# Causal attention rounds on GpSimd: the order of the feed-forward's square and gate, a mask, and the last step of the operand split

## The chip, the cores and the metric

The kernel runs on one core of a Trainium2 chip. The metric is the device time of one execution in microseconds (us), the median of several runs. The engines are TensorE (PE; PEld is its weight load), VectorE (DVE), ScalarE (ACT), GpSimd (POOL) and SyncE (SP), which here only issues transfers.

## The reference

An encoder-like block on x of 16 sequences, 256 tokens and 128 channels:

```python
x = x + 0.5 * L0_ffn(layernorm(x))      # r = sigmoid(xr @ W_r'), k = relu(xk @ W_k')**2, out = r * (k @ W_v')
x = x + L0_attn(layernorm(x))           # causal attention, 16 heads of 8 channels, softmax with clip and epsilons
x = x + 0.5 * L0_ffn(layernorm(x))
x = x + 0.5 * L1_ffn(layernorm(x))      # 8 experts, top 2
x = x + L1_attn(layernorm(x))           # 3 steps of a refined attention
x = x + 0.5 * L1_ffn(layernorm(x))
```

In L0_ffn, xr and xk are mixtures of each token with the one before it: x_prev + mu * (x - x_prev). Only the first three lines bear on the change: they are worked out together, sequence by sequence.

## The kernel before, in words

The first three lines of the block run as 16 **causal rounds**, one for each sequence n, with eight steps each, one for each pair of heads (`causal_round` in the program of every engine, called by `causal_steps`: rounds 0, 1 and 12 to 15 written out, 2 to 11 as a hardware loop of two rounds). Round n holds the attention of sequence n, the second feed-forward of sequence n - 2, the first feed-forward of sequence n + 3, and the preparation of operands of sequences n + 1 and n + 2. Each engine runs its own list strictly in order; what ties the lists together are semaphores. So the order in which the Python function of an engine calls its helpers is the order of its queue, and that order is written out by hand.

For one pair of heads TensorE computes the scores twice: `row_scores` (L1736, mask product L1747 and score products L1752) into ps_q, from which VectorE takes row maxima (`row_maxima`, L2622), and `causal_scores` (L1757) into ps_k, which ScalarE exponentiates (`causal_exps`, L1290). GpSimd then sets what lies above the diagonal to zero (`causal_keep`, L935, an affine select at L940). Behind every second pair TensorE multiplies with the values (`causal_values`, L1768, products L1778 and L1781), once the masks of its two pairs are done.

**The feed-forward** of one sequence passes through all engines. VectorE normalises (`ln_apply`, L2576), TensorE transposes (`tokens_t`, L1682), ScalarE copies to y_t, GpSimd takes the difference of neighbouring tokens (`mix_step`, L875), VectorE makes the two mixtures (`mix_inputs`, L2592 and L2593), TensorE multiplies (`ffn_hidden`, L1696 and L1698), ScalarE writes kr, the relu of k (L1192), and the logarithm for the sigmoid's denominator (L1194 to L1199). GpSimd squares kr (`mix_square`, L879, waits for kr) and adds the two parts of the logarithm (`mix_gate`, L884, waits for the Ln of L1199). TensorE multiplies the square with W_v (`ffn_out`, L1704, waits for the square), ScalarE's last exponential (L1203) waits for the gate, VectorE forms the product (`mix_gated`, L2599), GpSimd adds it to x (`mix_add`, L889). A flag `first` stands for the first feed-forward (rounds 0 to 12), `second` for the second (rounds 2 to 15).

**The operand split.** Queries and keys of the next sequence are needed as three bf16 parts. ScalarE rounds qk32 to part 0, GpSimd does the rest: `causal_parts` (rest = qk32 - part 0, L916; part 1 = rest rounded, L920) and `causal_last_parts` (part 2 = rest - part 1, L924). The last one raises `parts_ready`, for which SP waits in `causal_operands`: SP then issues one transfer of the query parts to DRAM (scr_q, L707), three of the key parts (scr_x, L710), and behind waits for those, six back into q_st (`query_halves`, L597) and two into k_st (`key_halves`, L605). TensorE's `row_scores` for pair 0 of round n + 1 waits for all eight of these (`fast_operands_in`). ScalarE's next write into parts, late in the round, waits for the outward transfers. Splits take place in rounds 1 to 14 (`parts_next`).

On VectorE the list around the change is: maxima of the fourth pair, `causal_normalise` (L2662 to L2668, ends with o_tok, which TensorE transposes behind the values of the second group), maxima of the fifth pair, `mix_inputs` of the second feed-forward (waits for GpSimd's step L875), `mix_gated` of the first (waits for TensorE's and ScalarE's results), `middle_normed` (y of sequence n + 2, L2576), maxima of the sixth pair. TensorE's transposes of that y are L1682 into ps_m.

Of the kernel before, what the change touches and what calls it, by code (L numbers as in the profile page):

```python
# [73 lines left out]
def macaron_kernel(nc, a, out):  # L74
    ctx = ExitStack()
    with ctx:
# [39 lines left out]
        def sem(name):  # L116
            if name not in made:
                made[name] = ctx.enter_context(nc.semaphore(name))
            return made[name]
# [271 lines left out]
        def within(n, low, high):  # L391

            return not isinstance(n, int) or low <= n <= high
# [13 lines left out]
        def mix1(f):  # L407
            return place(mix_order, 1, f, (2, -5))

        def mix2(b):  # L410
            return place(mix_order, 2, b, (2, 6))

        def norm1(f):
            return place(norm_order, 1, f, (3, -6))
# [4 lines left out]
        def norm3(b):  # L419
            return place(norm_order, 3, b, (3, 10))  # L420
# [393 lines left out]
        def _(pool):  # L814
# [53 lines left out]
            def hold():  # L868

                pool.sem_inc(sem("held"), 1)  # L870


            def mix_step(i, l):
                pool.wait_ge(sem("T_ytc"), l + 1)
                pool.tensor_tensor(dy[:, :], y_t[:, 1:T + 1], y_t[:, 0:T], ALU.subtract).then_inc(sem("F_dy"), 1)  # L875

            def mix_square(i):
                pool.wait_ge(sem("F_kr"), i + 1)
                pool.tensor_tensor(ka[:, :], kr[:, :], kr[:, :], ALU.mult).then_inc(sem("F_ka"), 1)  # L879

            def mix_gate(i):

                pool.wait_ge(sem("F_ln"), i * 3 + 3)
                pool.tensor_tensor(er[:, :], er[:, :], rec[:, :], ALU.add).then_inc(sem("F_sum"), 1)  # L884

            def mix_add(i, b):
                pool.wait_ge(sem("F_gated"), i + 1)
                hold()
                pool.tensor_tensor(x[:, b, :], x[:, b, :], gated[:, :], ALU.add).then_inc(sem("F_x"), 1)  # L889
# [23 lines left out]
            def causal_parts(f):  # L913

                pool.wait_ge(sem("part_hi"), f + 1)
                pool.tensor_tensor(rest[:, :, :], qk32[:, :, :], parts[:, :, 0, :], ALU.subtract)\  # L916
                    .then_inc(sem("part_rest"), 1)
                pool.wait_ge(sem("part_rest"), f + 1)
                hold()
                pool.tensor_copy(parts[:, :, 1, :], rest[:, :, :]).then_inc(sem("part_mid"), 1)  # L920

            def causal_last_parts(f):
                pool.wait_ge(sem("part_mid"), f + 1)
                pool.tensor_tensor(parts[:, :, 2, :], rest[:, :, :], parts[:, :, 1, :], ALU.subtract)\  # L924
                    .then_inc(sem("parts_ready"), 1)

            def causal_values(n, p):
                if not isinstance(n, int) or n >= 2:
                    pool.wait_ge(sem("fast_values"), (n - 1) * NGV + 2)
                pool.wait_ge(sem("G_vc"), n + 1 + 1)  # L930
                hold()
                pool.tensor_copy(v_heads(p)[:, :, :, 0:HD], v_tok[:, :, :, :].rearrange("p t (a s) d -> p (t a) s d", s=2))\
                    .then_inc(sem("fast_v"), 1)

            def causal_keep(n, hp):  # L935
                g, j = hp * 2 // HG, hp * 2 % HG
                pool.wait_ge(sem("fast_exp"), n * HP + hp + 1 + 2)
                hold()
                e = e_buf[g % 2][:, j:j + 2, 0:2 * P].rearrange("p u (c q) -> p u c q", c=2)
                pool.affine_select(out=e, in_=e, compare_op=ALU.is_ge, fill=0.0, base=0,  # L940
                                   pattern=[[0, 2], [0, 2], [1, P]], channel_multiplier=-1)\
                    .then_inc(sem("causal_kept"), 1)

            def causal_round(n, p, half):
                first, second, after = within(n, 0, B - 4), within(n, 2, B), within(n, 0, B - 2)
                parts_next = within(n, 1, B - 2)
                causal_keep(n, 0)
                if first:
                    mix_step(mix1(n + 3), norm1(n + 3))
                causal_keep(n, 1)  # L950
                if parts_next:
                    causal_parts(n + 1)
                causal_keep(n, 2)
                if parts_next:
                    causal_last_parts(n + 1)
                if first:
                    mix_square(mix1(n + 3))
                    mix_gate(mix1(n + 3))
                causal_keep(n, 3)
                if second:  # L960
                    mix_step(mix2(n - 2), norm3(n - 2))
                causal_keep(n, 4)
                if first:
                    mix_add(mix1(n + 3), n + 3)
                causal_keep(n, 5)
                if second:
                    mix_square(mix2(n - 2))
                    mix_gate(mix2(n - 2))
                causal_keep(n, 6)
                if after:  # L970
                    causal_values(n + 1, 1 - p)
                causal_keep(n, 7)
                if second:
                    mix_add(mix2(n - 2), n - 2)
# [19 lines left out]
            causal_parts(1)  # L994
            causal_last_parts(1)
            causal_steps(pool, causal_round)
            ffn(mix2(B - 2), norm3(B - 2), B - 2)
            ffn(mix2(B - 1), norm3(B - 1), B - 1)
# [2702 lines left out]
```

## Time and profile before

| | us |
|---|---|
| median of 3 runs | 1375.23 |
| lowest, highest | 1371.81, 1378.19 |
| the profiled execution | 1369.53 |
| its span, first to last instruction | 1367.8 |
| busy: PE, DVE, ACT, POOL | 1217.5, 920.0, 842.2, 533.9 |
| granted TensorE clock, mean share of full | 0.966 |

The busy times are sums over the whole span. The kernel has stages with different limits, so they say little about one stage; for that the waits and the timelines of a stretch are read. A timeline row has the start in us from the span's start, the duration, the engine, the line and the operation; in brackets stands how long the engine had been idle, and what released it. Neighbouring durations can overlap by some hundredths.

### The profile page before, as it was taken

Reading aid. Unit: us, or ns where it says so; the run is one execution under the profiler, and the core shown is the slowest. Engines: PE = TensorE matmul, PEld = TensorE weight load, DVE = VectorE, ACT = ScalarE, POOL = GpSimd, SP = SyncE. Lnnn points to the kernel's source line nnn. Section 1 sums busy time; section 2 is a strip of 40 time slices with the busy share of each in tenths; the row PEclk is TensorE's granted clock in tenths of the full one; section 3 lists DMA queues with packets and bytes.
Section 4 is the critical chain, followed back from the end, with each engine's and each line's share of the span. In section 5 each row is a group of like instructions: output and inputs, shape, how many; then the busy total and the mean of one; then the engine's idle time right before and its main releaser. Section 6 shows DMA issues by size and latency. Waiting matters only on the chain. (4 is left out here: it accounts for less than half of the span.)

```text
span 1367.8 us, 36731 instructions
## 1 busy us (share of the span) xinstructions
PE 1217.5 (89%) x12275; PEld 781.6 (57%) x12275; DVE 920.0 (67%) x2874; ACT 842.2 (62%) x1549; POOL 533.9 (39%) x817
## 2 busy tenths in 40 slices
PE   4689899898759999999889988999899997999998
PEld 3456566566537777777544433444344443767876
DVE  3578888887746874677677745666766665677444
ACT  3467777776433344443677877899787885333543
POOL 6366766766430040401344433344333331032344
PEclk9799999999959999999999999999999999999999
DMA  6323323324204022111545544445434441001332
GB/s 162 93 66 93 97 58 104 92 64 106 53 7 139 3 76 84 55 32 52 142 120 155 151 126 113 144 137 141 126 111 126 122 119 39 1 28 41 102 115 85
DMA packets 113582, 125.77 MB, mean 92 GB/s; under 512 B 14988, under 2 KB 90020, under 8 KB 113450
## 3 DMA queue, kind: packets, MB, share of 16 engines
q1 hardware_dynamic: 110378, 117.82, 30.6%
q0 software_dynamic: 3072, 6.30, 1.5%
q8 instruction: 69, 1.13, 0.3%
q14 instruction: 63, 0.52, 0.1%
HBM read 79.89 MB, written 44.05 MB: 91 GB/s over the span
## 5 line engine op out<-in xcount | busy, mean ns | idle before, releaser
L1469 ACT ACTIVATE e_buf<-ps_q 128x1024 f32<-128x1024 f32 x192 | 196.9, 1026 | 58.0 <-PE ps_q L2194 57.7
L2207 PE MATMUL ps_o<-e_buf,v_st 128*32 128x256 f32 x3072 | 210.7, 393 | 5.1 <-POOL v_st L1081 4.2
L1469 ACT ACTIVATE e_buf<-ps_k 128x1024 f32<-128x1024 f32 x192 | 197.0, 1026 | 7.5 <-PE ps_k L2194 7.4
L2054 PEld LDWEIGHTS ps_o<-w,e_buf 128*128 128x128 f32 x1280 | 152.2, 193 | 13.1 <-issue 12.0
L2054 PE MATMUL ps_o<-w,e_buf 128*128 128x128 f32 x1280 | 158.4, 277 | 0.0
L2622 DVE TENSOR_REDUCE mx<-ps_q 128x10 f32<-128x640 f32 x128 | 104.9, 820 | 45.0 <-PE ps_q L1752 44.1
L1290 ACT ACTIVATE e_buf<-ps_k 128x768 f32<-128x768 f32 x128 | 103.0, 805 | 46.2 <-PE ps_k L1764 45.3
L2207 PEld LDWEIGHTS ps_o<-e_buf,v_st 128*32 128x32 f32 x3072 | 81.5, 110 | 76.6 <-issue 40.3
L940 POOL TENSOR_SCALAR_AFFINE_SELECT e_buf<-e_buf 128x512 f32<-128x512 f32 x128 | 85.6, 669 | 89.8 <-ACT e_buf L1290 86.9
L1385 ACT ACTIVATE e_buf<-ps_q,b_t 128x512 f32<-128x512 f32 x80 | 54.6, 685 | 90.5 <-PE ps_q L2046 86.7
L1385 ACT ACTIVATE e_buf<-ps_k,b_t 128x512 f32<-128x512 f32 x80 | 54.0, 685 | 71.0 <-PE ps_k L2046 67.6
L2194 PE MATMUL ps_q<-q_st,k_st 64*128 64x256 bf16 x768 | 76.6, 278 | 19.9 <-DMA q_st<-scr_q 15.8
L2194 PE MATMUL ps_k<-q_st,k_st 64*128 64x256 bf16 x768 | 75.4, 275 | 5.4 <-ACT e_buf L1469 3.1
L1039 POOL DMA_INDIRECT slots_in<-heads_out,vp_all x40 | 39.7, 991 | 101.0 <-DVEq L3526 89.6
L2194 PEld LDWEIGHTS ps_q<-q_st,k_st 64*128 64x128 bf16 x768 | 22.3, 94 | 99.2 <-ACT e_buf L1469 62.6
L1088 POOL TENSOR_TENSOR rest<-qk,parts 128x256 f32<-128x256 f32 x48 | 32.6, 680 | 112.9 <-DVE parts L3141 112.9
L2046 PE MATMUL ps_q<-mix,w 128*128 128x512 f32 x144 | 70.1, 610 | 2.4 <-issue 2.4
L1747 PE MATMUL ps_q<-mask_d,ident_b 64*64 64x128 bf16 x512 | 57.6, 232 | 13.6 <-DVE mx L2622 8.4
L2046 PE MATMUL ps_k<-mix,w 128*128 128x512 f32 x144 | 68.0, 594 | 0.0
L3125 DVE COPY y_t<-ps_m 128x256 f32<-128x256 f32 x48 | 20.3, 423 | 70.0 <-PE ps_m L1682 69.7
L2898 DVE SCALAR_TENSOR_TENSOR e_buf<-ps_o,lexp,e_buf 128x128 f32<-128x128 f32 x160 | 44.8, 342 | 33.0 <-PE ps_o L2054 30.2
L1752 PE MATMUL ps_q<-k_st,q_st 64*64 64x256 bf16 (+3 forms) x1024 | 67.0, 235 | 0.0
(392 smaller groups left out, 2746.5 us busy)
## 6 DMA issues: line engine op xcount, KB each, us to landing
k_st<-scr_x SPq DMA_DIRECT2D x128, 256.0 KB
q_st<-scr_q SPq DMA_DIRECT2D x256, 96.0 KB
scr_q<-parts SPq DMA_DIRECT2D x64, 192.0 KB, 2.0
scr_x<-parts SPq DMA_DIRECT2D x48, 192.0 KB, 2.0
q_st<-scr_q SPq DMA_DIRECT2D x128, 64.0 KB
slots_in<-heads_out SPq DMA_DIRECT2D x3, 1536.0 KB
slots_out<-heads_out SPq DMA_DIRECT2D x18, 256.0 KB
heads_out<-slots_in SPq DMA_DIRECT2D x15, 256.0 KB
```

What stands on the lines that cost most here:

```text
L940: pool.affine_select(out=e, in_=e, compare_op=ALU.is_ge, fill=0.0, base=0, pattern=[[0, 2], [0, 2], [1, P]], channel_multiplier=-1)\
L1290: act.activation(e_buf[g % 2][:, hp * 2 % HG:hp * 2 % HG + 2, 0:3 * P], ps_k[:, :, 0:3 * P], ACT.Exp, bias=SHIFT).then_inc(sem("fast_exp"), 1)
L1385: act.activation(h_sb[e % 2][:, f, :], bank, ACT.Relu, bias=b1_t[:, j:j + 1])\
L1469: act.activation(e_buf[g % 2][:, hp * 2 % HG:hp * 2 % HG + 2, :], (ps_q, ps_k)[hp % 2][:, :, :], ACT.Exp).then_inc(sem("fast_exp"), 1)
L1747: mm(o[at, own[0]:own[1] + 1:own[1] - own[0], :], ident_b[at, at], mask_d[at, :, :], start=True, stop=False, tile_position=(u * RH, u * RH ...
L1752: last = mm(ps_q[at, bank, seg * RH:(seg + j + 1) * RH], q[at, hp, j * RH:(j + 1) * RH], k[at, hp, 0:(j + 1) * RH], start=False, stop=True ...
L2046: mm(bank, w1[:, e, f * P:(f + 1) * P], mixed(m, u)[:, :], start=True, stop=True)\
L2054: last = mm(ps_o[:, e % 2, t * P:(t + 1) * P], h_sb[e % 2][:, f, t * P:(t + 1) * P], w2[:, e * NF + f, :], start=f == 0, stop=f == NF - 1)
L2194: last = mm(bank[:, u, t * T:(t + 1) * T], k_st[p][at, h, t * P:(t + 1) * P], q_st[p][at, h, :], start=True, stop=True, tile_position=(64 ...
L2207: last = mm(ps_o[at:at + VW, p, low:low + T], v_st[p][:, kt, h, :], e_buf[g % 2][:, j, kt * T:(kt + 1) * T], start=g == 0 and kt == 0, sto ...
L2622: red(mx[:, hp, :, :], ps_q[:, :, 0:SEGS * RH].rearrange("p b (s k) -> p b s k", k=RH), AX.X, ALU.max)\
L2898: last = stt(acc[u][:, t, :], ps_o[:, e % 2, t * P:(t + 1) * P], gate[u][:, t, e:e + 1], acc[u][:, t, :], ALU.mult, ALU.add)
```

## The change

In the rounds with a split (1 to 14) GpSimd's list between the third and the fourth pair's mask, and behind the latter, is put in another order. Before: mask 3, last part, square, gate, mask 4, step. After: mask 3, square, gate, mask 4, last part, step. No instruction is added, removed or altered, and no other engine's program changes. In rounds 13 and 14, which have no first feed-forward, mask 4 now stands ahead of the last part; in rounds 0 and 15, which have no split, nothing moves.

```diff
--- before.py
+++ after.py
@@ -951,12 +951,12 @@
                 if parts_next:
                     causal_parts(n + 1)
                 causal_keep(n, 2)
-                if parts_next:
-                    causal_last_parts(n + 1)
                 if first:
                     mix_square(mix1(n + 3))
                     mix_gate(mix1(n + 3))
                 causal_keep(n, 3)
+                if parts_next:
+                    causal_last_parts(n + 1)
                 if second:
                     mix_step(mix2(n - 2), norm3(n - 2))
                 causal_keep(n, 4)
```

## Rows read from the trace of the kernel before

**Rows 1.** Waits, 60 to 320 us: engine, line, releaser; us in total, times, longest.

```profile
PE ps_m L1704 <- POOL mix L879: 16.6, 12, 1.6
...
PEld ps_m L1682 <- DVE y L2576: 4.5, 18, 0.3
```

**Rows 2.** GpSimd's timeline in round 7: start, duration, line, operation [idle before, releaser].

```profile
202.72 0.68 POOL L940 TENSOR_SCALAR_AFFINE_SELECT e_buf<-e_buf 128x512 f32<-128x512 f32 x1
203.37 1.15 POOL L924 TENSOR_TENSOR parts<-rest,parts 128x512 bf16<-128x512 f32 x1
204.48 0.85 POOL L879 TENSOR_TENSOR mix<-mix 128x256 f32<-128x256 f32 x1
205.29 0.90 POOL L884 TENSOR_TENSOR mix<-mix 128x256 f32<-128x256 f32 x1
206.15 0.82 POOL L940 TENSOR_SCALAR_AFFINE_SELECT e_buf<-e_buf 128x512 f32<-128x512 f32 x1
206.94 0.60 POOL L875 TENSOR_TENSOR mix<-y_t 128x256 f32<-128x256 f32 x1
207.98 0.64 POOL L940 TENSOR_SCALAR_AFFINE_SELECT e_buf<-e_buf 128x512 f32<-128x512 f32 x1 [0.43 <-ACT e_buf L1290]
...
211.61 0.61 POOL L879 TENSOR_TENSOR mix<-mix 128x256 f32<-128x256 f32 x1 [0.70 <-ACT mix L1192]
213.06 0.73 POOL L884 TENSOR_TENSOR mix<-mix 128x256 f32<-128x256 f32 x1 [0.83 <-ACT mix L1199]
```

**Rows 3.** TensorE's timeline in round 7, and where rounds 8, 11 and 14 start.

```profile
205.47 0.71 PE L1704 MATMUL ps_m<-w_t,mix 128*128 128x128 f32 x4 [1.36 <-POOL mix L879]
...
207.03 0.64 PE L1781 MATMUL ps_o<-e_buf,v_st 128*32 128x256 f32 x8
...
209.79 0.44 PE L1682 MATMUL ps_m<-ident,y 128*128 128x128 f32 x2
...
216.65 0.24 PE L1747 MATMUL ps_q<-mask_d,ident_b 64*64 64x128 bf16 x2
...
278.67 0.24 PE L1747 MATMUL ps_q<-mask_d,ident_b 64*64 64x128 bf16 x2
...
339.22 0.24 PE L1747 MATMUL ps_q<-mask_d,ident_b 64*64 64x128 bf16 x2
```

**Rows 4.** VectorE's timeline in round 7.

```profile
204.45 0.41 DVE L2662 TENSOR_TENSOR corr<-s_du,vs 128x256 f32<-128x256 f32 x1
...
205.65 0.83 DVE L2668 TENSOR_TENSOR o_tok<-corr,s_rec 128x256 f32<-128x256 f32 x1
206.84 0.82 DVE L2622 TENSOR_REDUCE mx<-ps_q 128x10 f32<-128x640 f32 x1 [0.36 <-PE ps_q L1752]
207.58 0.48 DVE L2592 SCALAR_TENSOR_TENSOR mix<-mix,cols,y_t 128x256 f32<-128x256 f32 x1
...
209.15 0.59 DVE L2576 TENSOR_SCALAR y<-x,mv,rstd 128x128 f32 x2
```

**Rows 5.** ScalarE's timeline in round 7: Ln of the gate, exponential of pair four.

```profile
203.62 0.42 ACT L1199 ACTIVATE mix<-mix 128x256 f32<-128x256 f32 x1
203.94 0.79 ACT L1290 ACTIVATE e_buf<-ps_k 128x768 f32<-128x768 f32 x1
```

**Rows 6.** VectorE's timeline behind the last round: L2668 with GpSimd idle.

```profile
388.80 0.42 DVE L2668 TENSOR_TENSOR o_tok<-corr,s_rec 128x256 f32<-128x256 f32 x1
```

**Rows 7.** Stretches of 0.25 us: busy by engine, PEclk, share of DMA engines, GB/s.

```profile
213.25:213.50 0.25, 0.25 (x6) 0.16 (x8) 0.14 (x2) 0.25 (x1) 0.25 (x1) 1.00 0.03 0
276.00:276.25 0.25, 0.25 (x12) 0.12 (x6) 0.00 (x0) 0.24 (x1) 0.25 (x1) 1.00 0.01 0
338.00:338.25 0.25, 0.25 (x5) 0.25 (x4) 0.24 (x1) 0.25 (x1) 0.00 (x0) 1.00 0.08 33
726.25:726.50 0.25, 0.25 (x12) 0.09 (x4) 0.24 (x1) 0.25 (x1) 0.08 (x2) 1.00 0.02 0
```

**Rows 8.** TensorE's timeline in the later attention stage: a start behind transfers.

```profile
727.48 0.40 PE L2194 MATMUL ps_q<-q_st,k_st 64*128 64x256 bf16 x4 [0.66 <-DMA q_st<-scr_q]
```

## The prediction

> **What bounds the kernel now.** The change touches only the causal rounds, 16 of some 20.7 us each in a span of 1367.8 us, so I read that stretch alone. First the waits there: between 60 and 320 us TensorE stands idle 16.6 us in 12 pieces until GpSimd's square (L879) is done, and right behind it stands a second, much smaller wait, 4.5 us in 18 pieces, for VectorE's normed rows y [rows 1]. The first is the wait that the edit aims at; the second tells how near the next limit is. Then the engines one by one through one round of the loop (n = 7; round 8 starts at 216.65 and round 11 at 278.67, so 20.67 us each [rows 3]; pairs are counted from one, the third mask is `causal_keep(n, 2)`). GpSimd works without a gap from the third mask at 202.72 to the second step at 207.54: mask, last part, square, gate, mask, step [rows 2]. TensorE waits 1.36 us for the square, starts the value product at 205.47, the values of group two at 207.03, is at the transposes of y at 209.79, and from there on it is busy without a recorded wait to the next round's first scores at 216.65 [rows 3]. VectorE normalises until 206.48, reduces the scores at 206.84, starts mix_inputs at 207.58, which is 0.04 us after GpSimd's step ended, and has y ready at 209.74, 0.05 us before TensorE uses it [rows 2 to 4]. So what sets the second half of the round is a chain: GpSimd's unbroken row up to the step, mix_inputs, mix_gated, y, transposes. TensorE's wait for the square lies beside this chain, and ends in it.
>
> **The square and the gate, moved ahead.** The work on GpSimd is the same six instructions. The square can start at 203.37 instead of 204.48. Alone it takes 0.61 us, beside VectorE's work 0.85 [rows 2]; here it falls beside a reduction, where the last part took no longer either, so I take 0.61: end 203.98, and TensorE starts about 204.15, 1.3 us sooner. The gate needs ScalarE's Ln, which ends at 204.04 [rows 5]; other engines start 0.04 to 0.14 behind an end that they wait for (step to mix_inputs, square to product [rows 2 to 4]), so 204.12: GpSimd's row gets a new gap of 0.14. Gate 0.73 (at 213.06) to 0.90, I take 0.73, as it starts before VectorE's product at 204.45: end 204.85. The mask of pair four needs the exponential that ends at 204.73 [rows 5], so no wait; 0.64 (as the third's 0.68) to 0.82, I take 0.82: end 205.65.
>
> **The last part, moved behind the mask.** It starts at 205.6 and takes 1.15 to 1.35 (the other two-input operations got 0.17 to 0.24 longer beside VectorE), I take 1.26: end 206.86 instead of 204.52, **2.34 us later**. With everything short it is 0.61 + 0.14 + 0.73 + 0.64 = 2.1 later, with everything long 0.85 + 0.14 + 0.90 + 0.82 + 0.2 = 2.9. The step of the second feed-forward comes next: 0.60 to 0.78, end 207.5 to 207.65 against 207.54.
>
> **VectorE beside it.** Its product L2668 takes 0.42 alone [rows 6] and 0.83 when GpSimd is at work beside it [rows 4]; 205.65 plus 0.41 is 206.06, close to where the gate ends, so I read it as waiting for GpSimd's running instruction. In the new order that instruction is the long last part: L2668 would end near 207.1 instead of 206.48, the reduction near 207.9 instead of 207.66, and mix_inputs would start 0.1 to 0.25 late. Against that, the fifth mask, which starts at 207.98 today [rows 2] because its exponential is late, could run right behind the step: then it lies beside less of mix_inputs, which is 1.6 us from its start to y's [rows 4], and that takes back some tenths. I set this at 0 to 0.1 a round, between ends of -0.3 (no overlap anywhere) and +0.3. **So y does not come sooner**, and TensorE's 1.3 us turns into waits for the reduction (208.0) and for y (209.8). Expected gain of the moved square: nothing in rounds 2 to 12; in round 1, which has no second step, up to 1 us, if the next operands are there.
>
> **The transfers behind the last part.** This is the term that I think decides. parts_ready starts SP's twelve transfers: one to scr_q, three to scr_x, six back to q_st, two to k_st. TensorE's first scores of the next round wait for the last eight. No row shows the end of that wait, since it was never the last. I bound it: in round 7 the engines stop moving data at 213.3 [rows 7], 8.8 us behind the last part. How much later the wait is free shows in a later stage, where the same six and two transfers are the last thing awaited: data stops near 726.3, and TensorE starts at 727.48 [rows 7, 8], 1.15 us on. So the operands were usable at about 214.45 and used at 216.65: 2.2 us to spare, against a shift of 2.34. In round 10 data stops near 276.05 (usable 277.2) and the scores start at 278.67: 1.45 to spare [rows 3, 7]. The rest of the rounds lie between, most near the first. Lateness is then 0.15 to 0.9 a round, I take 0.3 on the mean of rounds 1 to 12; it is not won back, as the whole loop hangs on that start: 12 x 0.3 = 3.6 us. Round 1's possible gain is lost to the same wait. In rounds 13 and 14 there is no square; only the mask goes ahead, and the last part comes 0.8 to 1.0 later. Round 13 has nothing to spare: data stops near 338.2, usable 339.35, scores at 339.22 [rows 3, 7]; it pays 0.8. Round 14 is as the first, with room. ScalarE's next write to parts waits for the outward transfers alone, and comes only behind the seventh pair (GpSimd's gate at 213.06 lies ahead of it [rows 2]); at 2.3 us later they are still in by then, so I put it at nothing. If that cover went, the split of the round after next would start late, with most of a round to spare.
>
> The Trainium skill (DMA: Bandwidth & Descriptors, "Anatomy of one DMA", which is on GpSimd's path) puts the fixed part of a transfer at some 2.0 us and says that most of it is the write receipt. By that figure the operands would be usable at 215.3 and round 7 late by 1.0 us, as an estimate 12 us in all, which is the lower half of rival (a) below; the rows show 1.15 for the same transfers, and the sum goes by them.
>
> **Sum.** Square and gate 0; y chain 0.05 x 11 = 0.5; operands 3.6 + 0.8 = 4.4; round 1 another -0.6 before its operands bind. That is +4.3 us on the profiled execution's 1369.5 us, which lies 5.7 below the median of the runs; carried to the median, 1375.2 + 4.3 = **1379.5 us**. A measurement of this kernel can tell about 0.5% (6.9 us) from no change.
>
> **Rivals.**
> (a) *Operands truly late, slower.* The place is the first scores of each round. If the last part shifts by 2.9 (all of GpSimd's work beside VectorE's) against 2.2 to spare, or by 2.34 with the spare time of all rounds nearer to round 10's 1.45, each of 13 rounds pays 0.6 to 0.9 us, and up to 1.4 with both: +8 to +15, 1383 to 1390 us. It decides from a mean lateness of 0.53 us a round. For it: spare and shift are within 0.2 of each other, so every error on that side counts in full; against it: the row at 727.48. Chance 0.28.
> (b) *Nothing binds.* Shift 2.1, spare 2.2: operands just in time, y as before, +0 to -3 us: 1372 to 1377. Chance 0.24.
> (c) *The wait was the bound, faster.* If TensorE's 1.3 us passes through to y, 12 x 1.3 = 15.6 less: 1360 us. For it speaks only the size of the wait; against it the 0.04 us between step and mix_inputs and the 0.05 between y and the transposes. It needs the operands in time too. Chance 0.07, partial gains of over 0.5% included.
> My forecast (y chain unchanged, operands late by a little) has 0.41, with a range of its own of 1377 to 1383.
>
> **How the numbers follow.** Faster by over 0.5% is (c), 0.07. Slower by over 0.5% is (a), 0.28. The rest, 0.65, is within. The range runs from (b)'s lower part, with a margin for the 3 us by which single runs differ, to the middle of (a): 1370 to 1388.
>
> **What would show it.** Right: TensorE's wait for L879 gone or under 0.3 us; a wait of about 1 us before the transposes of y instead; mix_inputs still starting within 0.2 us behind L875; the last part ending 2.1 to 2.9 later in the round; a new wait "DMA q_st or k_st" before the first L1747 of most rounds, 0.1 to 0.9 us each; a period of 20.7 to 21.2. Wrong: a period under 20.4 (then y was not the limit), or no wait for operands at all with the last part 2.3 later (then the spare time was misread).

## The result, and the profile after

The median went from 1372.49 us (13 runs, 1366.87 to 1378.19) to 1381.40 us (13 runs, 1371.22 to 1388.51): ratio 1.0066, 95% interval 1.0043 to 1.0090, so 9 us slower, between 6 and 12. The profiled execution took 1376.49 us (span 1374.8) against 1369.53 (span 1367.8); both lie below the medians, the one after by 4.9. The forecast was 1379.5, in a range of 1370 to 1388. The three runs whose median of 1375.23 stands ahead of the prediction are among the 13. Here and below, "ratio" is the ratio on record with its 95% interval; it can differ by up to a quarter of a per cent from the quotient of two medians.

First the waits of the kernel after, 60 to 325 us (engine, line, releaser; us in total, times, longest). They answer to [rows 1].

```profile
PEld ps_q L1747 <- issue: 27.5, 75, 2.2
...
PE ps_m L1682 <- DVE o_tok L2668: 8.6, 12, 0.7
...
PE ps_q L1747 <- DMA k_st<-scr_x: 5.4, 8, 2.0
...
PE ps_m L1682 <- DVE y L2576: 3.7, 12, 0.8
...
PEld ps_m L1704 <- POOL mix L879: 0.7, 2, 0.5
...
PE ps_m L1704 <- POOL mix L879: 0.3, 1, 0.3
```

TensorE's 16.6 us for the square are down to 0.3 in one piece (1.0 with the weight loads), most of it in the stretch up to 100 us. In their place stand 8.6 us for o_tok and 3.7 for y, in every round, and a wait that the kernel before did not have: 5.4 us in 8 pieces until k_st has landed. The weight load ahead of the same line grew with it ("issue", longest 0.5 before and 2.2 now).

GpSimd's timeline in round 7 of the kernel after, which answers to [rows 2]. The round starts at 199.49; it started at 196.00 before, so 3.49 is taken off for a comparison.

```profile
206.75 0.61 POOL L879 TENSOR_TENSOR mix<-mix 128x256 f32<-128x256 f32 x1
207.37 0.73 POOL L884 TENSOR_TENSOR mix<-mix 128x256 f32<-128x256 f32 x1
208.16 0.71 POOL L940 TENSOR_SCALAR_AFFINE_SELECT e_buf<-e_buf 128x512 f32<-128x512 f32 x1
208.84 1.32 POOL L924 TENSOR_TENSOR parts<-rest,parts 128x512 bf16<-128x512 f32 x1
210.13 0.79 POOL L875 TENSOR_TENSOR mix<-y_t 128x256 f32<-128x256 f32 x1
210.87 0.63 POOL L940 TENSOR_SCALAR_AFFINE_SELECT e_buf<-e_buf 128x512 f32<-128x512 f32 x1
```

VectorE's and TensorE's timelines of the same round, answering to [rows 4] and [rows 3].

```profile
209.18 1.26 DVE L2668 TENSOR_TENSOR o_tok<-corr,s_rec 128x256 f32<-128x256 f32 x1
210.37 0.81 DVE L2622 TENSOR_REDUCE mx<-ps_q 128x10 f32<-128x640 f32 x1
211.10 0.68 DVE L2592 SCALAR_TENSOR_TENSOR mix<-mix,cols,y_t 128x256 f32<-128x256 f32 x1
...
212.44 0.59 DVE L2576 TENSOR_SCALAR y<-x,mv,rstd 128x128 f32 x2
```

```profile
207.49 0.71 PE L1704 MATMUL ps_m<-w_t,mix 128*128 128x128 f32 x4
...
210.50 0.44 PE L1682 MATMUL ps_m<-ident,o_tok 128*128 128x128 f32 x2 [0.72 <-DVE o_tok L2668]
211.33 0.24 PE L1747 MATMUL ps_q<-mask_d,ident_b 64*64 64x128 bf16 x2 [0.39 <-DVE mx L2622]
...
213.08 0.44 PE L1682 MATMUL ps_m<-ident,y 128*128 128x128 f32 x2 [0.26 <-DVE y L2576]
...
220.25 0.24 PE L1747 MATMUL ps_q<-mask_d,ident_b 64*64 64x128 bf16 x2 [0.24 <-DMA k_st<-scr_x]
```

From the round's own start, before and after:

| | before | after |
|---|---|---|
| square (L879) ends | 9.33 | 7.87 |
| last part (L924) ends | 8.52 | 10.67 |
| step (L875) ends | 11.54 | 11.43 |
| o_tok (L2668) ends | 10.48 | 10.95 |
| mix_inputs (L2592) starts | 11.58 | 11.61 |
| y (L2576) ends | 13.74 | 13.54 |
| next round starts | 20.65 | 20.76 |

The square comes 1.46 us sooner, and y comes 0.2 sooner: the gain stops between the two. The last part comes 2.15 later, and the next round now waits for the operands. In the records of the transfers one can read when the last of the eight that TensorE waits for has landed. Before, that was 1.78, 2.98, 1.96, 2.36, 2.29, 1.97, 2.38, 2.52, 2.33, 1.61, 2.16, 2.78, 0.39 and 2.84 us ahead of the next round's first matmul, for rounds 1 to 14. After, it is 0.14 to 0.25 in all of these rounds but 6 (1.62) and 14 (2.96): the operands have become what starts the round, and TensorE starts 0.14 to 0.25 us behind their landing.

Next rounds 1 to 3, 6 and 7 of the kernel after as stretches (length; busy PE, PEld, DVE, ACT, POOL; PEclk, share of the DMA engines, GB/s), then 13 and 14.

```profile
71.53:92.69 21.16, 17.03 (x243) 11.22 (x243) 16.52 (x45) 13.58 (x31) 11.45 (x16) 1.00 0.31 86
92.69:114.35 21.66, 18.72 (x254) 12.72 (x255) 17.68 (x48) 15.04 (x37) 14.25 (x20) 1.00 0.30 84
114.35:136.01 21.66, 18.73 (x254) 12.73 (x255) 17.62 (x49) 15.05 (x37) 14.22 (x20) 1.00 0.33 84
...
177.50:199.49 21.99, 20.21 (x255) 13.69 (x255) 17.77 (x48) 14.90 (x37) 14.41 (x21) 0.92 0.28 80
199.49:220.25 20.76, 18.73 (x256) 12.73 (x256) 17.44 (x51) 15.23 (x38) 14.24 (x21) 1.00 0.30 85
...
324.04:343.04 19.00, 16.48 (x244) 11.29 (x244) 14.63 (x41) 12.51 (x28) 11.39 (x17) 1.00 0.34 95
343.04:365.38 22.34, 19.12 (x237) 12.40 (x236) 16.20 (x47) 10.68 (x24) 10.60 (x16) 0.77 0.30 81
```

And of the kernel before, rounds 1 to 3, 13 and 14.

```profile
71.60:91.75 20.15, 18.20 (x243) 11.69 (x242) 15.37 (x44) 12.79 (x28) 11.56 (x16) 0.92 0.33 90
91.75:113.36 21.61, 19.82 (x256) 13.34 (x255) 16.81 (x49) 15.16 (x37) 13.09 (x19) 0.92 0.30 84
113.36:134.00 20.64, 18.71 (x255) 12.69 (x254) 17.76 (x50) 15.23 (x37) 14.36 (x21) 1.00 0.32 88
...
320.58:339.22 18.64, 16.56 (x244) 11.30 (x244) 14.27 (x41) 12.50 (x28) 11.35 (x17) 1.00 0.39 97
339.22:359.99 20.77, 17.07 (x237) 11.48 (x237) 15.49 (x47) 10.69 (x24) 10.63 (x16) 0.92 0.34 87
```

A common round is hardly longer (rounds 7 to 11: 20.71 on the mean against 20.66), but rounds 1 to 3 together are 64.48 against 62.40, and of the three of after, all at full clock, two are almost a whole microsecond over the common round. Stretches at half clock (1.2 GHz; PEclk 0.92 is one of 3.4 us in a round) fall in rounds 1, 2 and 14 before, in 6 and 14 after; a round with one is 1.0 to 1.3 us longer. Round 15 starts at 365.38 against 359.99: 5.4 of the span's 7.0 us arise in the causal rounds. Rounds 6 and 14, the two of after in which the operands were not late, give 2.9 of these 5.4: both have half clock, round 14 for 10.2 us where it had 3.4 before. So this one profile does not by itself show that late operands cost the time; the experiments do. Of the other 1.6 us, 0.9 arise in round 15, which has a stretch at half clock of 6.8 us where the kernel before has one of 3.4 (both have a longer one at its end); the rest lies in later stages, which the change does not touch.

### The profile page after: what moved, and what is told of

Same layout as the page of the kernel before. It is cut to its first block and busy times, and to the rows that moved or that the text cites. A ratio compares the mean times of both kernels' runs of the same rounds, so it can differ in the third digit from the quotient of the medians.

```text
span 1374.8 us, 36731 instructions
## 1 busy us (share of the span) xinstructions
PE 1219.7 (89%) x12275; PEld 783.1 (57%) x12275; DVE 923.1 (67%) x2874; ACT 840.1 (61%) x1549; POOL 532.4 (39%) x817
## 3 DMA queue, kind: packets, MB, share of 16 engines
q8 instruction: 70, 1.15, 0.4%
## 5 line engine op out<-in xcount | busy, mean ns | idle before, releaser
L2194 PE MATMUL ps_q<-q_st,k_st 64*128 64x256 bf16 x768 | 76.7, 278 | 21.4 <-DMA q_st<-scr_q 17.4
L1747 PE MATMUL ps_q<-mask_d,ident_b 64*64 64x128 bf16 x512 | 57.9, 232 | 22.4 <-DVE mx L2622 11.7
L3125 DVE COPY y_t<-ps_m 128x256 f32<-128x256 f32 x48 | 20.4, 424 | 71.4 <-PE ps_m L1682 71.0
```

Of the source, the lines that this page charges most:

```text
L1747: mm(o[at, own[0]:own[1] + 1:own[1] - own[0], :], ident_b[at, at], mask_d[at, :, :], start=True, stop=False, tile_position=(u * RH, u * RH ...
L2194: last = mm(bank[:, u, t * T:(t + 1) * T], k_st[p][at, h, t * P:(t + 1) * P], q_st[p][at, h, :], start=True, stop=True, tile_position=(64 ...
```

## The experiments

The theory going in: late operands. The loss is the operand transfers, which start 2.15 us later, and the square's wait was worth nothing, because GpSimd's list up to the step, mix_inputs and y bound the round. The rivals: a stretched product (the loss is VectorE's L2668, 0.83 before and 1.26 us after, and what follows it), and an eaten gain (the square's gain is real, and the transfers take it back and more). A third rival, that the changed order brings more stretches at half clock, has no run of its own; the clock records speak to it in part, as said below. e1 to e4 ran on one chip with the kernel before at 1370.26 us. e6 to e13 ran on another, on which the later stages take longer (in e12 round 15 starts at 359.82, and the span is 1442.3), with the kernel before at 1447.16 (e6 to e9) and 1441.83 (e10 to e13); each ratio is to the kernel before on its own chip.

### e1_square_first: the square sooner, the last part nearly where it was

```diff
                 causal_keep(n, 2)
+                if first:
+                    mix_square(mix1(n + 3))
                 if parts_next:
                     causal_last_parts(n + 1)
                 if first:
-                    mix_square(mix1(n + 3))
                     mix_gate(mix1(n + 3))
```

> Edit: before's order, with the square alone moved ahead of the last part (mask 3, square, last part, gate, mask 4, step). Theory 'operands late' (T): TensorE's wait for the square falls from 16.6 us to under 5, the last part ends only 0.6 to 0.85 us later and the spare time before each round's first scores (1.5 us or more in rounds 1 to 12, round 13 unchanged) still covers it; the step L875 ends when it did, so y and the round stay: period 20.6 to 20.7, ratio to before 0.998 to 1.002. Rival 'the wait was the bound': 1.1 us a round less, ratio 0.990 or lower.

Measured: 1370.97 us, ratio 1.0007 (0.9988 to 1.0026). Its round 7 starts at 194.54. GpSimd's timeline:

```profile
201.91 0.61 POOL L879 TENSOR_TENSOR mix<-mix 128x256 f32<-128x256 f32 x1
202.48 1.15 POOL L924 TENSOR_TENSOR parts<-rest,parts 128x512 bf16<-128x512 f32 x1
203.59 0.91 POOL L884 TENSOR_TENSOR mix<-mix 128x256 f32<-128x256 f32 x1
```

VectorE's:

```profile
202.99 0.93 DVE L2663 TENSOR_TENSOR corr<-s_du,vs 128x256 f32<-128x256 f32 x1
...
204.81 0.74 DVE L2669 TENSOR_TENSOR o_tok<-corr,s_rec 128x256 f32<-128x256 f32 x1
205.47 0.81 DVE L2623 TENSOR_REDUCE mx<-ps_q 128x10 f32<-128x640 f32 x1
```

and TensorE's:

```profile
202.66 0.71 PE L1705 MATMUL ps_m<-w_t,mix 128*128 128x128 f32 x4
...
205.33 0.64 PE L1782 MATMUL ps_o<-e_buf,v_st 128*32 128x256 f32 x8 [1.19 <-POOL e_buf L940]
...
208.42 0.44 PE L1683 MATMUL ps_m<-ident,y 128*128 128x128 f32 x2 [0.44 <-DVE y L2577]
```

The value product starts 8.12 us into the round instead of 9.47, with no wait, and the transposes of y start at 13.88, where they were at 13.79. TensorE waits for the fourth mask instead (1.19 us; it had no recorded wait there), and then for y (0.44). The round is 20.74. VectorE shows why y does not come sooner. Before, it stood idle for 0.36 us ahead of its reduction for the fifth pair (the fifth reduction from here on), until TensorE's scores came [rows 4]. Here the scores are early, but the first product of `causal_normalise` runs under the last part and takes 0.93 us instead of 0.41, the products end 0.53 later in the round, and the reduction follows them with no idle time. So the square's 1.35 us are gained on TensorE and lost again before y. Late operands are not in play from round 2 on (they land 1.2 to 1.9 us ahead of the next start in rounds 2 to 11); only the start of round 2 waits for them. So there is no gain in the loop that the transfers could have eaten.

### e2_transfers_late: the order before, and SP also waits for the fourth mask

```diff
             def causal_operands(f, p, half):
                 sp.wait_ge(sem("parts_ready"), f + 1)
+                if not isinstance(f, int) or f >= 2:
+                    sp.wait_ge(sem("causal_kept"), (f - 1) * HP + 4)
```

> Edit: before's order on GpSimd, but SyncE's wait for parts_ready is joined by a wait for the round's fourth mask (2.45 us behind the last part's end), so that only the operand transfers start later, by about what the change makes them later. T: the loss of the change appears with nothing else altered, +4 to +10 us, ratio 1.003 to 1.008, waits 'DMA' before the first L1747 of most rounds. Rival 'VectorE beside the last part' (L2668 stretched to 1.26 us, o_tok and the reduction late): nothing of it is in this kernel, ratio 1.000 within 0.1%.

Measured: 1376.32 us, ratio 1.0055 (1.0035 to 1.0075). Its waits, 60 to 325 us:

```profile
PE ps_m L1706 <- POOL mix L881: 17.0, 12, 1.6
...
PE ps_q L1749 <- DMA k_st<-scr_x: 5.3, 9, 1.5
```

All compute instructions stand in the order of the kernel before (the square's wait is back, 17.0), and yet the same wait for k_st appears, 5.3 against the change's 5.4, and the same loss. The operands land 20.3 to 21.3 us into a round, the changed kernel's 20.4 to 21.4. With VectorE undisturbed this is the late start of the transfers alone; the stretched product isn't needed for the loss.

### e3_before_mask: the last part behind the gate, but ahead of the fourth mask

```diff
                 causal_keep(n, 2)
-                if parts_next:
-                    causal_last_parts(n + 1)
                 if first:
                     mix_square(mix1(n + 3))
                     mix_gate(mix1(n + 3))
+                if parts_next:
+                    causal_last_parts(n + 1)
                 causal_keep(n, 3)
```

> Edit: square and gate moved ahead as in the change, but the last part left in front of the fourth mask (mask 3, square, gate, last part, mask 4, step). The last part ends about 1.5 us later than before. T: the spare time of 1.5 to 2.8 us covers it in nearly all rounds, so ratio 0.999 to 1.002, with landings just in time in rounds 1 and 10. Rival 'VectorE beside the last part': L2668 still meets a longer GpSimd instruction, and half of the loss stays, ratio 1.003.

Measured: 1372.64 us, ratio 1.0030 (1.0012 to 1.0049), more than was expected. The last part ends 10.13 into the round, 1.6 later than before. In the profiled execution the operands of rounds 2 to 11 still land 0.4 to 0.9 us ahead of the next start, one round of the stretch waits for k_st (1.3 us, ahead of round 2), and the period is 20.68. So this profile does not show the loss that the median shows. With so little to spare, a landing that is late by a few tenths counts, and landings vary by more than that (9.65 to 10.55 behind the last part in one execution of the kernel before). That other executions have such landings is argued, not shown, and other executions may as well differ in their stretches at half clock.

### e4_fewer: the change, with four query transfers back instead of six

```diff
+            def query_fewer(p, landed):
+                for u in range(2):
+                    sp.dma_start(q_st[p][64 * u:64 * u + 48, 0:HP, :].rearrange("r h t -> r (h t)"),
+                                 bass.AP(scr_q.tensor, p * 3 * PLANE + u * HP * T, [[0, 2], [H * T, 24], [1, HP * T]]))\
+                        .then_inc(landed, 16)
...
-                query_halves(p, sem(f"fast_operands_in_{p}"))
+                query_fewer(p, sem(f"fast_operands_in_{p}"))
```

> Edit: the changed kernel, but the six transfers back into q_st are four in the causal rounds (the first two copies of the parts in one transfer), the same bytes. SyncE issues two fewer at 0.39 us each. T: operands land 0.4 to 0.8 us sooner and most of the loss goes: ratio to before 1.000 to 1.003, against the change's 1.0066. Rival 'VectorE beside the last part': the loss stays, 1.006. Rival 'bytes, not issues, set the chain': landings unmoved and the loss stays too; the two are told apart by when the data stops.

Measured: 1490.52 us, ratio 1.0875 (1.0842 to 1.0909): a miss by a wide margin. TensorE waits 52.8 us for k_st:

```profile
PE ps_q L1757 <- DMA k_st<-scr_x: 52.8, 8, 7.8
```

The transfers between 200 and 218 us, as tenths of the 16 engines in 40 slices of 0.45 us, and what they moved:

```profile
DMA  0499995017123099988401111111111110000000
GB/s 0 127 311 325 339 337 163 0 18 164 46 100 109 36 264 273 191 164 200 109 27 46 55 55 55 55 55 55 46 55 46 55 36 18 0 0 0 0 0 0
```

Behind the burst runs a tail of some 12 slices at a tenth of the engines and 55 GB/s, which is 5.4 us. A tenth is about 2 of 16, and the new transfers have a source whose outermost dimension is 2. The Trainium skill (DMA: Bandwidth & Descriptors, "Why a DMA increments its semaphore by 16 and not by 1") says that such a transfer uses the largest number of engines, up to 16, that divides the outermost dimension of both sides: here 2. The trace agrees with its 0.1. Joining transfers this way makes them narrow.

### e6_keys_early: the change, with two of three outward key transfers sent behind part 1

```diff
+                sp.wait_ge(sem("part_mid"), f + 1)
+                hold()
+                key_part(0)
+                key_part(1)
                 sp.wait_ge(sem("parts_ready"), f + 1)
...
-                for j, n in enumerate(PARTS):
-                    sp.dma_start(scr_x[f].rearrange("(i c t) -> c i t", c=C, t=T)[:, 3 * j:3 * j + n, :],
-                                 parts[:, 1, j, :].unsqueeze(1).broadcast_to([P, n, T])).then_inc(sem("k_parts_out"), 16)
+                key_part(2)
```

> Edit: the changed kernel, but SyncE issues the first two of the three outward key transfers as soon as their parts are there (behind L920, a wait for part_mid), and only scr_q and the third behind the last part. Same transfers, same bytes. T: two issues of 0.53 us leave the chain behind the last part, so operands land 0.8 to 1.1 us sooner (9.8 becomes about 8.8 us behind the last part), the spare time turns from 0 to about 1 us in the loop, and the loss of the change goes: ratio to before 0.999 to 1.002, no wait 'DMA' before L1747 but in single rounds. Rival 'the loss sits on GpSimd and VectorE': ratio stays 1.005 to 1.007.

Measured: 1452.67 us, ratio 1.0033 (1.0018 to 1.0048), where the change itself gives 1.0065 on the same chip (e11). GpSimd's list is the changed one, so VectorE is disturbed as there; only transfers moved. The operands land 9.1 to 9.8 us behind the last part instead of 9.7 to 10.8, and the wait for k_st falls from 8 pieces to one:

```profile
PE ps_q L1752 <- DMA k_st<-scr_x: 1.6, 1, 1.6
```

By the two ratios half of the loss is back, though their intervals overlap. The gain of 0.5 us a round in the landing was half of what I had expected, and so was the effect (0.999 to 1.002). What remains is not explained by this profile: round 15 starts at 363.92, 4.1 us later than in e12, and rounds 12 to 14, whose operands land 1.8 to 3.0 us ahead, are longer than e12's by 5.2 us together, with 13.7 us at half clock against 3.4.

### e7_keys_first, e8_step_first, e9_old_order

e7 is e6 with the two transfers into k_st issued ahead of the six into q_st:

```diff
-                sp.wait_ge(sem("parts_out"), f * 16 + 32)
-                hold()
-                query_halves(p, sem(f"fast_operands_in_{p}"))
                 sp.wait_ge(sem("k_parts_out"), f * 48 + 96)
                 hold()
                 key_halves(p, f, sem(f"fast_operands_in_{p}"))
+                sp.wait_ge(sem("parts_out"), f * 16 + 32)
+                hold()
+                query_halves(p, sem(f"fast_operands_in_{p}"))
```

> Edit: as e6_keys_early, and the two large transfers into k_st are issued ahead of the six into q_st. T: the data of the large two then moves under the issues of the six; landings 7 to 8 us behind the last part, 2 us or more to spare, ratio 0.998 to 1.001; no further gain over e6 but in rounds whose landing varied. If the period of the loop stays at 20.66 with 2 us to spare, the limit is the chain of GpSimd's step, mix_inputs and y.

Measured: 1457.27 us, ratio 1.0074 (1.0047 to 1.0102), a miss: the operands land 10.0 to 11.2 behind the last part, later than in e6. TensorE's wait is now for q_st:

```profile
PE ps_q L1752 <- DMA q_st<-scr_q: 10.5, 10, 3.0
```

The group that is issued last is the one that TensorE waits for. In this order the queries stand behind SP's wait for the last outward key transfer, which is a likely cause, not a tested one; the first inward issue comes 2.6 us behind the last part in round 7 against 2.2 in e6, which is less than half of the delay.

e8 puts the step ahead of the last part in e7 (mask 3, square, gate, mask 4, step, last part), to test whether the step is what y waits for:

```diff
                 causal_keep(n, 3)
-                if parts_next:
-                    causal_last_parts(n + 1)
                 if second:
                     mix_step(mix2(n - 2), norm3(n - 2))
+                if parts_next:
+                    causal_last_parts(n + 1)
```

> Edit: as e7_keys_first, and on GpSimd the step of the second feed-forward stands ahead of the last part (mask 3, square, gate, mask 4, step, last part). Theory 'y chain' (the round's second limit is GpSimd's step -> mix_inputs -> y): the step ends about 1.3 us sooner, mix_inputs starts behind the reduction, y comes 0.3 to 0.5 us sooner, period 20.2 to 20.4, ratio 0.995 to 0.998. Rival: period unchanged at 20.66, ratio 1.000.

Measured: 1471.24 us, ratio 1.0175 (1.0143 to 1.0208), a miss. The step ends 1.3 us sooner in a round of the loop, mix_inputs starts 0.5 sooner and y ends 0.2 sooner than in the changed kernel. So it is VectorE's own list that mix_inputs follows: in every version read (before, after, e1, e8) it starts some 0.08 us ahead of the recorded end of the fifth reduction. In the kernel before, the step ended within 0.12 us of that, so its rows could not tell the two apart. The last part ends 0.75 us later still (11.42 in a round) and the wait for operands nearly doubles against e7:

```profile
PE ps_q L1752 <- DMA q_st<-scr_q: 19.5, 11, 2.5
```

This is the late operands again, at a greater shift. VectorE's timeline of e8 in round 8, which starts at 227.55, shows what mix_inputs then follows:

```profile
237.88 0.81 DVE L2627 TENSOR_REDUCE mx<-ps_q 128x10 f32<-128x640 f32 x1
238.61 0.64 DVE L2597 SCALAR_TENSOR_TENSOR mix<-mix,cols,y_t 128x256 f32<-128x256 f32 x1
239.17 0.85 DVE L2598 SCALAR_TENSOR_TENSOR mix<-mix,cols,y_t 128x256 f32<-128x256 f32 x1
```

The reduction ends at 238.69 and mix_inputs runs right behind it; its second half now takes 0.85, as it lies under the fifth mask (238.92 to 239.74), where it took 0.47 in e1.

e9 is the order of before with e7's transfers.

> Edit: before's order on GpSimd with the transfers of e7_keys_first. T: operands 4 to 5 us to spare, which nobody needs: ratio 0.998 to 1.001, the only round that can gain is 13 (0.25 to spare before). A gain of over 0.3% would mean that landings cost before's kernel something in most runs that its one profile does not show.

Measured: 1449.19 us, ratio 1.0008 (0.9990 to 1.0026). The period is 20.65 to 20.70 in rounds 3 to 11, but for round 5, which has a stretch at half clock. The operands land 0.9 to 3.5 us ahead of the next start, and only 0.3 in round 13; 4 to 5 to spare were expected. The same transfers that cost e7 0.7% cost nothing that can be measured with the last part where it was.

### e10_transfers_later: e2 with the fifth mask, 1.65 us later still

```diff
                 sp.wait_ge(sem("parts_ready"), f + 1)
+                if not isinstance(f, int) or f >= 2:
+                    sp.wait_ge(sem("causal_kept"), (f - 1) * HP + 5)
```

> Edit: as e2_transfers_late, but SyncE waits for the fifth mask of the round instead of the fourth (1.65 us later again). Nothing else differs from the kernel before. T: no spare time is left in any round, so all of the 1.65 us counts 12 to 13 times: +20 us over e2, ratio to before 1.017 to 1.023. If the loss came from anything but the landing of the operands, the slope would be under half of that.

Measured: 1476.35 us, ratio 1.0215 (1.0189 to 1.0242), inside what was expected. The waits:

```profile
PE ps_q L1749 <- DMA k_st<-scr_x: 24.6, 10, 5.4
```

and rounds of 22.4 to 25.7 us in the loop. Against e2 it is 1.6% more, some 23 us, for a start of the transfers that is 1.65 us later: 1.8 us in each of 13 rounds. Once the operands bind, the shift passes in full. (e2 ran on the first chip, and the profiled execution of e10 was the slowest of its six.)

### e11_change_again: the change unaltered, beside e10, e12 and e13

> The changed kernel once more, unaltered, so that its profile and time stand beside e10 and e12 on one chip. T: ratio 1.004 to 1.009 again; every round's period is the offset of the last part's end plus the landing (9.7 to 10.8 us) plus 0.1 to 0.3, whatever the chip.

Measured: 1454.11 us, ratio 1.0065 (1.0039 to 1.0091): the same as on the first chip. In its profile most rounds are 20.6 to 21.1, and three (2, 9 and 14) have stretches at half clock, round 2 the longest:

```profile
92.92:116.69 23.77, 21.42 (x254) 14.36 (x255) 17.31 (x48) 14.98 (x37) 13.83 (x20) 0.86 0.27 77
```

In round 2 the stretch of 6.8 us lies ahead of the last part, which ends 13.2 us into the round instead of 10.7, and the operands land that much later. So where the operands bind, time lost at half clock ahead of the last part passes on to the next start. Round 15 starts at 366.49, 6.5 us later than in the kernel before on the first chip (the second has no profile of it; in e12 it is 359.82); the two profiled executions of the change give +5.4 and +6.5.

### e12_old_keys_early and e13_square_keys_early: is there anything to be had?

e12 is the kernel before with e6's edit of the transfers, e13 is e1 with it; both without change to the rest.

> Edit: before's order on GpSimd with the transfers of e6_keys_early (two outward key transfers issued behind part_mid). T: operands land about 0.5 us sooner, which only round 13 and rounds with a late landing can use: ratio 0.998 to 1.001.

Measured: 1443.61 us, ratio 1.0013 (0.9992 to 1.0033). The operands land 2.1 to 4.1 us ahead of the next start in rounds 2 to 12, and the period is 20.65 to 20.68 in rounds 3 to 11 (21.82 in round 4, with half clock): more room for them is worth nothing.

> Edit: e1_square_first with the transfers of e6_keys_early. T: TensorE's wait for the square is gone and the operands are in time, and still the loop's period stays at 20.6 to 20.75, because the step, mix_inputs and y have not moved: ratio 0.998 to 1.002. Rival 'the wait was the bound, only masked by late operands': 0.990 to 0.993.

Measured: 1441.89 us, ratio 0.9993 (0.9967 to 1.0020). The square's wait is gone and the operands of rounds 2 to 12 land 1.6 to 2.4 us ahead of the next start, so neither of the two known costs is left, and the period is 20.75, 0.1 more than before. A wait for the fourth mask stands where the square's stood, and one for y behind it:

```profile
PE ps_o L1787 <- POOL e_buf L945: 14.5, 12, 1.3
...
PE ps_m L1688 <- DVE y L2582: 5.7, 12, 1.0
```

The first of these was 0.5 us in all in e12.

Only round 1, which has no second step, is shorter (19.10 against 20.14 in e12), and there e12 has a stretch at half clock, and e13's next start waits for operands, so how much of it is the square isn't known. No version that ran beats the kernel before.

## Why the prediction was right or wrong

**The forecast as a whole.** It lies 1.9 us from the measured median, and part of that is luck. The 4.3 us of the sum were added to a median of three runs that lies 2.7 above that of 13; the difference itself is 8.9, about twice the sum, and 4.3 lies outside its interval of 6 to 12.

**The square and the gate: right in size and value, wrong in the reason.** The wait for L879 fell from 16.6 to 0.3 (with the weight loads 1.0), the square took the 0.61 that was set, and TensorE started 1.35 us sooner (1.3 set). The value of that is nil, as e1 and e13 show by themselves. But "TensorE's wait for the square lies beside this chain" is not how the kernel before runs: VectorE's fifth reduction, at 206.84, waited for scores that TensorE computes behind the square's product ([rows 4], 0.36 us idle), and mix_inputs follows that reduction as closely as it does the step. Two paths ended within 0.12 us of each other. The change clears the one through TensorE, and VectorE's longer products take its place.

**The last part: nearly right.** It ends 2.15 us later in a round, where 2.34 was set; mask 4 took 0.71 instead of 0.82, and the gate followed the square with no gap of 0.14. Its own 1.32 lay at the upper end.

**VectorE beside it: right.** L2668 ends 10.95 into the round; "end near 207.1" is 11.1. mix_inputs starts 0.03 later than before, and y ends 0.2 sooner, since mask 5 starts ahead of mix_inputs, as named for the take-back: its two halves take 0.68 and 0.47 instead of 0.48 and 0.90. So the 0.05 a round that were added are -0.2, within the ends that were set. What the prediction did not name is TensorE's wait for o_tok (8.6 us in total); it lies inside the time that was to be waited for y.

**The operands: the mechanism right, the size too small.** The spare time of the rounds that I read was right: 2.2, 1.45 and 0 us were set for rounds 7, 10 and 13. The landings give 2.38, 1.61 and 0.39, less the 0.14 to 0.25 that TensorE needs behind a landing. The Trainium skill (DMA: Bandwidth & Descriptors, "Anatomy of one DMA") gives the 2.0 us fixed part for the path on which GpSimd issues; by it round 7 would have 1.35 to spare. Here SP issues, and the landings do not bear it out. (The 12 us that the prediction worked out from it are the upper half of rival (a), not the lower.)

The step that was too small is "The rest of the rounds lie between, most near the first. Lateness is then 0.15 to 0.9 a round, I take 0.3 on the mean". If each round's operands had landed as far behind the last part as before, the measured shifts would make rounds 1 to 12 late by some 3 us in all, as an estimate from the landings, so the 3.6 were not small for typical landings. The changed kernel lost 3.5 us over rounds 1 to 12 in its profile, and 5.8 in e11's. That the 3.5 equals the sum's terms for these rounds (0.5 + 3.6 - 0.6) is a coincidence, since 1.3 of it is round 6, whose operands were in time and which has a stretch at half clock. The median's difference is 9, between 6 and 12. Two things were left out. First, a landing is not the same from round to round and from execution to execution: in rounds 1 to 3 it came 10.25 to 10.76 us behind the last part, 10.10 to 10.21 before, and these three rounds cost 2.1 us. Once nothing is to spare, each late one counts in full, and an early one gives back next to nothing (the shortest round that the operands start is 20.60). Most of that lateness is one issue. In rounds 2 and 3 SP issued the second transfer into k_st 1.47 and 1.63 us behind the first, where it is 0.70 elsewhere in the loop; from that issue to the landing it took 4.07 and 3.88 us, as in rounds 4 to 7 (3.79 to 3.96). Here are the two issues, merged, in rounds 3 and 4:

```profile
130.25 2.11 SPq L605 DMA_DIRECT2D k_st<-scr_x  x2
...
151.90 1.17 SPq L605 DMA_DIRECT2D k_st<-scr_x  x2
```

Second, the prediction has no term for stretches at half clock. In rounds 1 to 14 they come to 10.2 us before, 13.7 after and in e11, 17.1 in e2, 3.4 in e1 and e13, but 20.5 in e9, which lost nothing; at this size no order is to be seen. With longer waits for operands there is more: 27.3 in e8, 30.7 in e10, and 95.6 in rounds 1 to 11 of e4, every one of which has some. So whether the change's short waits bring more of them stays open. e2, which moves the transfers alone, has 1.0055, and its interval overlaps the change's: nothing beside the later start of the transfers is needed for the loss, but how it divides between waiting and half clock isn't settled.

**The rivals.** The measured ratio lies on the side of rival (a), "Operands truly late, slower", by its point estimate (over 0.5%), with an interval that begins at 0.43%. Its condition, a mean lateness of 0.53 us a round, isn't met in the profiled execution (3.5 us over 12 rounds) and about met in e11's (5.8). It had 0.28, and what spoke for it (spare and shift within 0.2 of each other) deserved more than that: between two such terms the outcome is not symmetric, as only lateness counts. (b) "Nothing binds" is excluded by the new wait. (c) "The wait was the bound" is excluded by e1 and e13 as a price for taking the wait away in these orders, in which VectorE's products get longer; no run takes it away without that.

**The signs.** Of those named, the wait for L879, mix_inputs within 0.2 us behind L875 (0.18: 210.92 to 211.10), the last part 2.1 to 2.9 later, and the wait for the operands all came. The second says less than was meant: mix_inputs starts 0.18 behind the step and right behind the reduction. The waits for y were less than the microsecond named, 0.26 in round 7, as o_tok and the reduction took their part first. Four rounds had a period over the 21.2 named (2, 3, 6 and 14), and the longest of the waits for operands was 2.0 where 0.9 was named.

**What stays open.** Some 0.7 us of the span's 7.0 lie behind round 15 and were not traced. The loss of e3 shows in its median alone, and the remaining loss of e6 lies in rounds whose operands were in time. Why SP's second issue comes late in rounds 2 and 3 isn't known; the share of busy DMA engines there (0.30 and 0.33) is that of the other rounds.

## What to carry to other kernels

Before an engine's list is put in another order, look at what the moved instruction releases beside compute: here a step of 1.2 us on an idle-looking engine was the start of twelve transfers with 10 us of latency. A stall that is large and regular can still be worth nothing. Before pricing its removal, read what the stalled engine waits for next (here the fourth mask and y), and what the moved instructions will now run beside (here VectorE's products, 0.41 us before and 0.93 in e1). And where a move takes all of the spare time of a transfer, price it by the worst landings and not by the typical one: the spare time is a reserve against their spread.

## What the runs showed of the hardware

- A VectorE instruction with two operands in SBUF that starts under or with a GpSimd instruction, and alone would end sooner, ends 0.26 to 0.29 us behind the latter. L2668 took 0.42 alone [rows 6], 0.83 under the gate [rows 2, 4], and 1.26 under the last part (12 of 12 rounds, 1262 to 1269 ns); the first product of `causal_normalise` took 0.41 before and 0.93 under the last part in e1. It holds the other way too: a GpSimd instruction that starts while such a VectorE instruction runs takes 0.07 to 0.24 us longer. The last part went from 1.15 to 1.32 where it starts (208.84) under VectorE's L2666 (208.67 to 209.15). The Trainium skill (SBUF — State Buffer, "Who interferes with whom") says that a VectorE instruction with two SBUF inputs contends with a GpSimd instruction that reads SBUF, that the shared ports are an exclusive lock, and that the order of issue decides which of the two blocks. Both numbers agree with it.
- A transfer whose source has an outermost dimension of 2 ran at a tenth of the engines and 55 GB/s, and the last landing came 16 us behind the last part instead of 10 (e4), as the rule cited there would have it.
- Sending two outward key transfers 4 us sooner brought the last landing only 0.5 us forward (e6), and issuing the inward ones in the other order put it back by about 1.0 (e7).
- Two transfers into k_st that SP issues one behind the other are 0.70 us apart in most rounds of the loop, and 1.47 and 1.63 in two of them (after, rounds 2 and 3); the last landing moves with the second issue.
- Stretches at half clock are more where TensorE waits long for operands: 95.6 us in rounds 1 to 11 of e4, against 10.2 in rounds 1 to 14 of the kernel before.
